# Attention on one core: the values' products of two rounds in one visit of the column tiles

## The reference, cut to what matters

```python
# 32 heads of 32, 8 groups of keys and values, 4 heads share a group
q = (x @ Wq)                                  # per head 1024 x 32
k, v = the halves of (x @ Wkv)                # per group 1024 x 32
scores = q @ k.T, -inf above the diagonal
weights = softmax(scores / sqrt(32))
ctx = weights @ v
y = ctx @ Wo + bo
```

## Time and profile before

| | |
|---|---|
| median of the runs | 2220.77 us |
| the profiled execution's own time | 2222.39 us |
| its span | 2220.3 us |
| attention's 16 passes | 975.0 to 1743 us of the span |
| mean granted TensorE clock | 0.973 |

### The profile page before, as it was taken

One profiled execution on the slowest core, in us unless ns is written; L12 is line 12 of the kernel. 1 busy time (PEld: TensorE's weight loads), 2 busy tenths in 40 slices (PEclk: granted clock), 3 DMA queues, 4 the chain that ended last, 5 costly groups with the idle time before them and its releaser, 6 DMA issues.

```text
span 2220.3 us, 30914 instructions
## 1 busy us (share of the span) xinstructions
PE 2057.5 (93%) x10568; PEld 1494.3 (67%) x10568; DVE 1411.5 (64%) x3276; ACT 955.2 (43%) x1990; POOL 997.1 (45%) x866
## 2 busy tenths in 40 slices
PE   5889987999999989989999999899998999999998
PEld 4645446788888879755556555555553688888887
DVE  6877766676776763387665677576768555544533
ACT  5755685232333323135554555455555332322311
POOL 1444586444444420018875586768873233120000
PEclk9999998999999999999999999999988999999999
DMA  6400275122211147422223723322223465544432
GB/s 186 172 2 29 101 248 213 39 76 77 74 67 68 68 173 272 121 53 55 68 71 100 212 66 78 78 77 72 52 68 121 137 225 174 167 161 138 134 117 92
DMA packets 148028, 249.78 MB, mean 112 GB/s; under 512 B 27150, under 2 KB 79246, under 8 KB 147648
## 3 DMA queue, kind: packets, MB, share of 16 engines
q1 hardware_dynamic: 136864, 227.89, 32.6%
q10 hardware_dynamic: 11008, 19.93, 2.9%
HBM read 140.01 MB, written 76.02 MB: 97 GB/s over the span
## 4 chain that ended last, share of the span: by engine, by line
PE 56%; POOL 15%; DVE 8%; issue 4%; DMA 3%; ACT 3%; SPq 1%; ACTq 1%; POOLq 0%; DVEq 0%
POOL c_S L2418 8%; PE PS L2609 4%; PE PS L2613 4%; PE PS L2610 4%; PE PS L1127 3%; PE PS L1126 3%; PE PS L1128 3%; PE PS L1986 3%; PE PS L1968 2%; PE PS L2001 2%; PE PS L1159 2%; PE PS L1161 2%; PE PS L1160 2%; DVE PS L2310 2%; PE PS L1944 2%
## 5 line engine op out<-in xcount | busy, mean ns | idle before, releaser
L2155 ACT ACTIVATE c_P<-PS 128x512 f32<-128x512 f32 (+3 forms) x768 | 357.3, 494 | 318.9 <-PE PS L1986 298.7
L1968 PE MATMUL PS<-c_K,c_Q 96*128 96x512 f32 (+3 forms) x768 | 276.2, 370 | 19.7 <-DVE cst L2310 13.9
L1986 PE MATMUL PS<-c_Q,c_K 97*128 97x512 f32 (+3 forms) x768 | 281.2, 380 | 7.0 <-DMA c_Q<-c_mT 4.3
L2418 POOL TENSOR_TENSOR c_S<-c_S,c_P 128x2048 f32<-128x2048 f32 (+3 forms) x94 | 272.7, 2901 | 8.6 <-ACT c_P L2155 0.2
L1986 PEld LDWEIGHTS PS<-c_Q,c_K 97*128 97x128 f32 x768 | 147.0, 194 | 174.4 <-ACT c_P L2155 97.2
L2306 DVE TENSOR_REDUCE cst<-PS 128x1 f32<-128x512 f32 x256 | 175.9, 687 | 91.4 <-PE PS L1968 91.0
L1968 PEld LDWEIGHTS PS<-c_K,c_Q 96*128 96x128 f32 x768 | 150.0, 196 | 75.0 <-DVE cst L2310 37.7
L2001 PE MATMUL PS<-c_P,c_V 128*32 128x512 f32 (+3 forms) x1536 | 168.2, 510 | 15.9 <-ACT c_P L2155 9.1
L2310 DVE CUSTOM_DVE_ANT_0 PS<-PS,maskw,cst 128x128 f32<-128x128 f32 (+3 forms) x256 | 142.8, 558 | 58.2 <-PE PS L1968 42.1
L213 POOL TENSOR_TENSOR maskw<-maskw,mhalf 128x1 f32<-128x1 f32 x64 | 38.6, 602 | 306.9 <-DVE maskw L171 297.9
L1259 ACT ACTIVATE b_g<-PS 128x460 f32<-128x460 f32 x96 | 53.0, 554 | 272.5 <-PE PS L1133 272.5
(11 more groups left out here) (301 smaller groups left out, 4887.8 us busy)
## 6 DMA issues: line engine op xcount, KB each, us to landing
a_xin<-in_x SPq DMA_DIRECT2D x32, 512.0 KB, 4.6
d_x<-scr SPq DMA_DIRECT2D x32, 512.0 KB, 4.8
c_Q<-c_qh SPq DMA_DIRECT2D x240, 64.0 KB, 2.0
scr<-a_xin SPq DMA_DIRECT2D x16, 512.0 KB, 6.7
b_xn<-scr SPq DMA_DIRECT2D x16, 512.0 KB, 5.7
b_x<-scr SPq DMA_DIRECT2D x16, 512.0 KB, 4.8
scr<-b_x SPq DMA_DIRECT2D x16, 512.0 KB, 2.6
scr<-b_y SPq DMA_DIRECT2D x16, 512.0 KB, 3.0
```

The costliest lines, as they stand in the source:

```text
L1968: e.matmul(bank[:, 0:hi - lo], self.Q4[0:96, 4 * (o % 3) + g, 128 * t:128 * t + 128], self.K4[0:96, HEADS[o % 8], lo:hi], start=True, stop ...
L1986: e.matmul(self.k.bank(i % 3)[:, 0:hi - lo], self.K4[0:97, HEADS[o % 8], 128 * kt:128 * kt + 128], self.Q4[0:97, 4 * (o % 3) + g, lo:hi], ...
L2155: e.activation(self.P[:, R % 3, g, 0:hi - lo], self.k.bank(i % 3)[:, 0:hi - lo], ACT.Exp, scale=SCALE).then_inc(self.exp_s.s, 1)
L2418: e.tensor_tensor(S[:, :, 512 - n:512], S[:, :, 512 - n:512], P[:, :, 0:n], ADD).then_inc(self.psum_s.s, 1)
```

## The change

Values' products are issued in every second round only, in the slot with g = 1 of odd rounds, two rounds at a time: those of R - 3 and of R - 2. The sum of a pass's first half moves from slot 20 to 21, where it stands behind products. Its bank turns are moved along, in BY_ROUND passes from slot 9 to 13. ACT's copy of the first half's sum goes behind the exponential of slot 22.

```diff
-                if o in BY_ROUND and s == 9:
+                if o in BY_ROUND and s == 13:
                     kept = turn(o, 49)
                 if o in BY_ROUND and s == 21:
                     keeps.append(kept)
-                if o not in BY_ROUND and s == 20:
+                if o not in BY_ROUND and s == 21:
                     keeps.append(turn(o, 49))
...
-                if g == 1 and S > 8:
-                    self.pe_pv(e, *divmod(S // 4 - 2, 12))
+                if g == 1 and r % 2 and S > 8:
+                    for R in (S // 4 - 3, S // 4 - 2):
+                        self.pe_pv(e, *divmod(R, 12))
                 if s == 5 and o > 0:
                     self.pe_sum(e, 2 * o - 1)
-                if s == 20 and o not in BY_ROUND:
+                if s == 21 and o not in BY_ROUND:
                     self.pe_sum(e, 2 * o)
...
                 if s == 6 and o > 0:
                     self.act_evac(e, 2 * o - 1, 1)
+                self.act_exp(e, o, r, g)
                 if s == 22:
                     self.act_evac(e, 2 * o, 1)
-                self.act_exp(e, o, r, g)
```

## The result

The changed kernel took 2230.07 us (median of 10 runs, 2223.87 to 2233.68), the kernel before 2223.01 (10 runs, 2217.14 to 2226.91). The ratio is 1.003, with a 95% interval of 1.0018 to 1.0042: slower by 0.3%, some 6.7 us. The forecast was 2214.6 and faster; the time lies outside the range of 2205 to 2225. The kernel before came out 2.2 us above the 2220.77 of three runs that the forecast started from, so the fair comparison is of the two differences: -6.2 us forecast, +6.7 measured.

The account below looks back on a forecast made before the run. Usual passes were taken as bound by PE in the first leg, then DVE, then POOL's 23.9 us. Terms -2.7 - 0.9 - 2.3 + 0 + 1.1 - 0.9 - 0.5 = -6.2 gave 2214.6 us from 2220.77; range 2205 to 2225.

Parts of the forecast that it names:

- The price of a visit: Entering and leaving a visit of products on PE costs 0.28 us; 107 visits go, 30 us of PE time.
- the first leg: Usual pass, slot 5's sum to slot 17's split: PE alone runs these 12.6 us; one visit less, about -0.3 us.
- the other legs: Usual pass, DVE's additions, then POOL's 23.9 us: both engines full, so a faster PE waits and gains nothing.
- the 3 us of cover for the exponential of slot 20: Usual pass, second leg: this exponential now waits for round 2's products, but DVE's additions come some 3 us later.
- The nine usual passes, -2.7: Passes 1, 2, 3, 6, 7, 10 to 13: -0.3 us each, bounds 0 and -0.6, together -2.7.
- the clock's case: Rival: less PE work near slot 25 halves the clock, 14 us over eleven passes, 2229; 0.16 shared with late exponentials.
- Pass 4, -2.3: Pass 4 up to slot 34: fewer visits, round 6's products leave, bank waits shrink; -2.3 us, bounds -1.1 and -3.3.
- Pass 8, +1.1: Pass 8: round 2's products and the sum now stand behind slot 21's wait; +1.1 us, bounds 0 and +2.
- Passes 0 and 9, -0.9 each: Pass 0: products come ahead of the wait for POOL; pass 9: slots 17 to 21 lose two visits; -0.9 us each.
- Passes 14 and 15, -0.5: Last two passes: merged visits save 0.28, ACT waits about as long; -0.5 us, bounds +2 and -3.
- the rival "eaten": Late exponentials or maxima cancel the usual passes' gain and half of pass 4's; -1.9 us, 2219; chance 0.22.

Follow-up runs that it names:

- late_early: Kernel before, with passes 14 and 15 alone joining products of rounds 5 and 6, 7 and 8, 9 and 10 in slots 30, 38 and 46; ratio 1.0002.
- late_only: Kernel before, with the change made in passes 14 and 15 alone; ratio 1.0030.
- usual_only: Kernel before, with the change made in the nine usual passes (1, 2, 3, 6, 7, 10 to 13) alone; ratio 0.9999.
- usual_fill: As usual_only, with the score matmuls of slots 17 to 24 of the nine usual passes issued twice; ratio against the kernel before 1.0016.
- fill_only: Kernel before, no visits joined, with score matmuls issued twice in parts of passes 0, 4, 8, 9 and 13 to 15; ratio 1.0006.

## Why the prediction was wrong

**The price of a visit and the first leg**: right. 0.3 us in a usual pass with a full clock, nothing from the other legs (9.93 and 23.95 us), and the 3 us of cover for the exponential of slot 20 held.

**The nine usual passes, -2.7**: wrong in the total, by the rival's mechanism. The step that failed is taking -0.3 as it stands while the clock's case was a rival at 0.16, one case for eleven passes or none. It came in 11 of 18 passes, with 3.4 or 6.8 us each. The size was off as well: the rival had 1.3 us for 6.8 us at half clock and room for 4.2 us; measured were -0.3 to 0.0 at 3.4 us (46.14 to 46.52) and +0.6 to +0.8 at 6.8, 1.0 us above the joined pass at full clock. By place it was right: the stretch with 11 matmuls holds slots 23 to 27, and the half clock began 24 to 28 us into each of the eleven. Result: 0.9999 in place of 0.9988, and in the profiles of the nine passes +1.9 and -2.05 us in place of -2.7.

**Pass 4, -2.3**: right (61.00 to 58.69) wherever its usual 3.4 us of half clock stayed away; with them -0.9 or less. **Pass 8, +1.1**: not seen; in the one profile that can be compared, joined takes what unjoined takes at the same half clock. **Passes 0 and 9, -0.9 each**: no profile has them joined at full clock (6.8 to 13.7 us at 0.50), so the terms stay open; the five passes together, forecast -3.0, measured +1.8 us, -1.8 to +5.6.

**Passes 14 and 15, -0.5**: this is the step that failed, +6.7 us (+3.6 to +9.8), beyond even my bound of +2. I had written that a two-round visit keeps ACT waiting about as long as two visits. It doesn't. The even round's products now stand behind waits that they used to stand ahead of: in pass 14 ACT waits 2.62 us for those of slot 21, and slots 12 to 20 take 11.2 to 11.6 us in place of 8.0 to 8.9. PE and ACT hand three score banks to and fro. Beside a single visit of 0.97 us ACT still has exponentials to run, and 0.54 us is left bare; of a double one more is bare (1.41 us at full clock, 3.10 at half, in late_early). I also priced every visit as 8 products and took the sums by round of these passes into no term: two rounds of them are 32 matmuls, 4.9 us in pass 15. And these passes ran partly at half clock before (14.4 and 6.1 us), where a visit takes longer (eight products of 512 columns 1.94 us against 1.06), and get more of it: pass 15 has 8.4 to 14.8 us at half clock in the kernels that change it, 0.5 to 6.6 in those that don't. No run holds the clock in passes 14 and 15 with the visits joined. By an estimate from the mean granted clocks (late_only 0.9693, before 0.9703, standard errors 0.0004), late_only loses 2.2 us of PE's work to it, 1.3 either way, so the clock can hardly be the whole 6.7.

Added up, 0.9999, 1.0008 and 1.0030 make 1.0037, with an interval of about 0.0026 either way, against 1.003. That the clock's rival said 2229 and 2230.07 was measured is luck: its 14 us were meant for eleven passes, of which usual_only shows about 2.5 (-0.2 in place of -2.7), and the loss came from passes 14 and 15. (The sum of the rival "eaten" leaves out the -0.5 of these passes; with it 2218.4 in place of 2219, which changes nothing.) What stays open: how the 6.7 us divides between lateness, length and the clock (3.1 for lateness unjoined, intervals overlapping), and what usual_fill lost outside its own passes.

## What to carry to other kernels

Joining two stretches of one engine's work saves its entry cost only where that engine alone sets the pace. Joining means that the earlier stretch is done later: look at what it stood ahead of, and whether it now stands behind a wait. Where two engines hand buffers to and fro, keep the pieces no longer than what the other has in hand, and count whatever stands in the piece (sums too), at the clock that this stretch really has. Before taking work out of a stretch in which PE already waits, look at the granted clock behind similar stretches; a few repeated matmuls there can cost less than the half clock they prevent. Change the passes that gain, and leave the ones that don't.

## What the runs showed that was not expected

Identical code has very different passes from run to run by where the clock falls: unchanged pass 8 took 59.12 to 62.30 us, unchanged pass 14 41.85 to 45.75. The kernel before ranged from 2214.9 to 2226.7 us over 23 runs, nearly three times the 4.4 us that count as a difference. A difference of two profiles in such a pass can't be put down to the edit. It can where unchanged code is steady: 53 of 56 unjoined usual passes (3 and 13 left out) took 46.44 to 46.57 us, and slots 28 to 44 of pass 15 took 9.56 to 9.59. And a higher granted clock that is bought with repeated work need not be less time: fill_only raised the mean by 0.004 and gained nothing.
